# A graph layer on one core: the table of mean and rstd stored sooner, three gathers behind rstd, b_edge's products ahead of the attributes'

## What is computed

```python
h    = relu(layernorm(x))                         # mean and rstd of each row of x
edge_emb = edge_attr @ W_edge + b_edge
msg  = relu(h[src] + edge_emb)
aggr = segment_sum(msg, dst)
h1 = (1 + eps) * h + aggr
h1 = gelu(layer_norm(h1 @ W1 + b1)); h1 = gelu(layer_norm(h1 @ W2 + b2))
h1 = layer_norm(h + h1)
out = x + layer_norm(h1 + gelu(h1 @ M1) @ M2)
```

## Time and profile before

| | |
|---|---|
| median of three runs | 529.01 us |
| the profiled execution | 530.68 us |
| its span | 528.7 us |
| PE, DVE, ACT, POOL busy | 473.1, 392.8, 309.4, 282.0 us |
| head, up to the first z | 0 to 32.2 us |
| edge stage, first to last z | 32.2 to 276.5 us |
| node stages | some 280 to 528 us |

### The profile page before, as it was taken

The page is one execution under the profiler, slowest core; times in us unless marked ns, Lnnn a source line. Parts: engine busy times, 40 slices in busy tenths (PEclk is TensorE's granted clock), DMA queues, the critical chain, the costliest instruction groups (busy, mean ns, idle before and its releaser), DMA issues.

```text
span 528.7 us, 7255 instructions
## 1 busy us (share of the span) xinstructions
PE 473.1 (89%) x1930; PEld 345.0 (65%) x1930; DVE 392.8 (74%) x563; ACT 309.4 (59%) x584; POOL 282.0 (53%) x295
## 2 busy tenths in 40 slices
PE   1398998999689997799687999999999999999994
PEld 0034655666446664466455888888888889888884
DVE  7953969999478995768696577777999866672575
ACT  5643767998558986766893556555666656013000
POOL 5575776777758777667500344534554463330252
PEclk9999998999979999799999999999999999999999
DMA  8966877777767767667404733243551132130122
GB/s 272 332 181 190 304 265 246 232 244 221 210 213 217 226 213 239 187 195 242 133 9 137 264 91 116 92 160 99 159 160 40 61 86 73 40 116 4 40 80 80
DMA packets 31716, 85.52 MB, mean 162 GB/s; under 512 B 4880, under 2 KB 5216, under 8 KB 31648
## 3 DMA queue, kind: packets, MB, share of 16 engines
q0 software_dynamic: 12688, 41.17, 25.8%
q1 hardware_dynamic: 18960, 43.52, 25.2%
HBM read 72.08 MB, written 5.25 MB: 146 GB/s over the span
## 4 chain that ended last, share of the span: by engine, by line
PE 39%; DVE 28%; issue 9%; ACT 7%; another core or an unknown queue 5%; POOL 3%; DMA 3%; ACTq 3%; DVEq 2%; POOLq 0%; SPq 0%
DVE msg_lo L1084 12%; DVE z L1078 11%; PE ps_u L1282 8%; PE ps_u L1284 8%; PE ps_u L1283 8%; PE ps_t L1282 3%; PE ps_t L1284 3%; PE ps_t L1283 3%; PE ps_t L1455 2%; ACT msg_hi L769 2%; ACT apart L685 2%; DMA w_raw<-in_W 2%; PE ps_u L1295 2%; DVEq L1077 1%
## 5 line engine op out<-in xcount | busy, mean ns | idle before, releaser
L574 POOL DMA_INDIRECT rows<-gather_table,src_idx x153 | 169.9, 1110 | 63.6 <-issue 43.6
L769 ACT ACTIVATE msg_hi<-z 128x1024 fp32r<-128x1024 f32 (+1 forms) x79 | 82.6, 1046 | 39.2 <-DVE z L1078 24.1
L580 POOL TENSOR_TENSOR var_eps<-mv,eps_t 128x1 f32<-128x1 f32 x40 | 21.6, 539 | 144.4 <-ACT squares L827 86.0
L1078 DVE TENSOR_TENSOR z<-ps_u,rows 128x1024 f32<-128x1024 f32 (+1 forms) x53 | 64.3, 1213 | 43.3 <-remote 34.6
L1084 DVE SCALAR_TENSOR_TENSOR msg_lo<-z,msg_hi 128x1024 fp32r<-128x1024 f32 (+1 forms) x79 | 95.3, 1208 | 1.4 <-ACT msg_hi L769 0.8
L1299 PE MATMUL ps_u<-we_raw,attr_raw 128*128 128x512 f32 x130 | 69.7, 636 | 16.6 <-DVE z L1078 13.5
L1317 PE MATMUL ps_t<-msg_lo,onehot 128*128 128x512 f32 x149 | 65.6, 440 | 4.8 <-ACT ps_t L728 3.6
L1282 PE MATMUL ps_u<-w_hi,lhs_lo 128*128 128x512 f32 x160 | 64.5, 403 | 1.0 <-DVE lhs_lo L1126 1.0
L1284 PE MATMUL ps_u<-w_hi,lhs_hi 128*128 128x512 f32 x160 | 62.6, 392 | 0.0
L1283 PE MATMUL ps_u<-w_lo,lhs_hi 128*128 128x512 f32 x160 | 62.3, 390 | 0.0
L1317 PE MATMUL ps_t<-msg_hi,onehot 128*128 128x512 f32 x149 | 59.7, 401 | 0.0
(11 more groups left out here) (178 smaller groups left out, 1015.1 us busy)
## 6 DMA issues: line engine op xcount, KB each, us to landing
attr_raw<-in_attr_t SPq DMA_DIRECT2D x20, 512.0 KB
w_raw<-in_W SPq DMA_DIRECT2D x24, 256.0 KB, 3.0
tile_in<-mid SPq DMA_DIRECT2D x10, 512.0 KB, 3.6
res<-in_x SPq DMA_DIRECT2D x20, 256.0 KB, 2.7
xin<-in_x SPq DMA_DIRECT2D x5, 512.0 KB, 6.1
out<-work SPq DMA_DIRECT2D x10, 256.0 KB, 2.0
rows<-gather_table,src_idx POOLq DMA_INDIRECT x153
gather_table<-tab SPq DMA_DIRECT2D x4, 512.0 KB
```

The costliest lines, as they stand in the source:

```text
L574: g.indirect_dma_start(rows[:, group.r, e % TPG, :], None, gather_table[:, :], bass.IndirectOffsetOnAxis(src_idx[:, e:e + 1].bitcast(u32), ...
L769: a.activation(pair(msg_hi, g, p), summed(g, p), ACT.Relu).then_inc(msg_hi_done, 1)
L1078: v.tensor_tensor(summed(g, p), embedded(g, p), rows[:, g.r, 2 * p:2 * p + g.in_pair(p), :].rearrange("p a d -> p (a d)"), ALU.add).then_i ...
```

## The change

SP stores `node_stats` behind the second store of the table instead of the third. DVE makes `x_nbias` and `x_pair` behind tile 4 of the table instead of tile 6 (with their waits for all moments and all rstd). POOL gathers the first direct tile behind rstd of piece 1 as before, the other three behind the rstd of the last piece. ACT splits the first attributes ahead of the scale of `acc`, not behind it. PE makes the four products of `b_edge` in one go as soon as `b_edge` is there, ahead of its wait for `we_lo`, and the products of the attributes accumulate on them.

```diff
             for c in range(XC - 1):
                 save_tables(2 * c, 2)
-                if c == 2:
+                if c == 1:
                     sp.wait_ge(x_pair_ready, 1)
                     sp.dma_start(node_stats.rearrange("(p t) c -> p (t c)", p=P),
...
                 if c == 1:
                     pool.wait_ge(idx_in, 16)
-                if c >= 1:
-                    direct_rows(c - 1)
-
+                    direct_rows(0)
+
+            for e in range(1, DIRECT):
+                direct_rows(e)
             pool.wait_ge(stats_idx_ready, 1)
...
+            split_attr(fixed(0))
             act.wait_ge(eps1_ready, 1)
             act.wait_ge(x_rstd_done, XC)
             a.activation(acc_scale[:, :], x_rstd[:, :], ACT.Copy, scale=eps1[:, 0:1]).then_inc(acc_scale_ready, 1)
             act.wait_ge(acc_scale_ready, 1)
             act.wait_ge(nodes_ready, NT)
-            split_attr(fixed(0))
...
-                if i == 6:
+                if i == 4:
                     dve.wait_ge(x_moments, NT)
                     dve.wait_ge(x_rstd_done, XC)
...
                 o = embedded(g, p)
-                alone_in_bank = g.gr != 0 if isinstance(g.gr, int) else True
+                fresh = not (isinstance(g.gr, int) and g.gr == 0)
                 for e in range(g.in_pair(p) - 1, -1, -1):
-                    if not alone_in_bank:
-                        t.matmul(o[:, e * D:(e + 1) * D], ones[0:1, :], b_edge[0:1, :], start=True, stop=False)
...
             t.matmul(ps_t[0][:, 0:2 * ET], ones[:, :], span_diag[:, :], start=True, stop=True).then_inc(span_all_ready, 1)
+            pe.wait_ge(b_edge_in, 16)
+            for p in range(2):
+                for e in range(2):
+                    t.matmul(embedded(fixed(0), p)[:, e * D:(e + 1) * D], ones[0:1, :], b_edge[0:1, :], start=True, stop=True)
             pe.wait_ge(we_lo_ready, 1)
-            pe.wait_ge(b_edge_in, 16)
             embed(fixed(0), 0)
             embed(fixed(0), 1)
             embed(fixed(1), 0)
```

More of the change, by code:

```diff
@@ L1278, in _, with three @@
             t = nc.tensor
[L1280 to L1284, removed]
+            def three(o, lhs, cols, rhs, rcols, first, last, skip=False):
+                t.matmul(o, lhs[1][cols], rhs[0][rcols], start=first, stop=False, skip_group_check=skip)
+                t.matmul(o, lhs[0][cols], rhs[1][rcols], start=False, stop=False, skip_group_check=skip)
+                return t.matmul(o, lhs[0][cols], rhs[0][rcols], start=False, stop=last, skip_group_check=skip)
             def embed(g, p):
@@ L1299, in embed @@
                         last = t.matmul(o[:, e * D:(e + 1) * D], attr_raw[:, g.k, (2 * p + e) * P:(2 * p + e + 1) * P], we_raw[:, :],
-                                        start=alone_in_bank, stop=True)
+                                        start=fresh, stop=True, skip_group_check=not fresh)
                     else:
                         last = three(o[:, 0:D], (attr_hi[:, place, :], attr_lo[:, place, :]),
-                                     (slice(None), slice(part * P, (part + 1) * P)), (we_hi, we_lo), (slice(None), slice(0, D)), alone_in_bank, True)
+                                     (slice(None), slice(part * P, (part + 1) * P)), (we_hi, we_lo), (slice(None), slice(0, D)), fresh, True,
+                                     skip=not fresh)
                 last.then_inc(emb_done[p], 1)
```

## The result

The change made the kernel **slower**: 537.52 us (median of 4 runs, 532.06 to 538.61) against 529.17 us for the kernel before beside it (4 runs, 528.76 to 530.51), a ratio of 1.0116, 95% interval [1.0066, 1.0166]. The profiled execution took 538.05 us, its span 536.3 us against 528.7.

The account below looks back on a forecast made before the run. The prediction took the chain through PE's attribute products and a late PE signal at pair 3 to bound the head. Pair 3 starts 8.7 us sooner, within POOL's slack of 10.9: 529.01 - 8.7 = 520.3 us, range 515.3 to 524.8.

Parts of the forecast that it names:

- nothing behind pair 3 has a fixed time of its own: Edge stage: only POOL's gathers have a fixed time, so pair 3's gain of 8.7 us reaches the end.
- the price of POOL's three gathers is nothing: POOL's head: gathers run from 15 to 18.8 us, before the statistics arrive, covered even if each took 1 us more.
- PE's `b_edge` products: PE's head: four products of 2.0 us run from 13.0 to 21.0 us, and the attributes start at 21.4.
- 25.0, 28.4 and 31.4: PE's ends of pairs 0, 1 and 2 in us, instead of 29.8, 37.5 and 40.2.
- Row and rule: PE's clock: removing `b_edge` products from the run may bring 2.4 GHz sooner, pair 2 done 2 to 3 us earlier.
- Small table and store: Head: small store at 16.9 us, landed at 21.3; first statistics gather 22.0, first table gather 27.1, 2.4 us sooner.
- `begin` at 31.4: PE ahead of pair 3: `begin` starts when PE is free at 31.4 us; the plan's reading adds 0 to 2 us.
- If the late signal goes with PE's work: Pair 3: PE's late signal keeps its 7.05 us behind `begin`, so pair 3 starts at 41.1, 8.7 us sooner.
- rival A: Pair 3: late signal gone or harmless, start near 36 us, POOL caps the gain at 10.9: 518.1 us; chance 0.24.
- "no change" rival: Edge stage: a later release that goes by its own time swallows all the gain; chance 0.04.
- rival B: Late signals shift and take back part, or store and plan come late: 3 to 6 us gained, 523 to 526; chance 0.12.
- Rival C: Early edge stage: idle PE stays at the low clock, 2.6 us lost per pair, 533.3 us with five; chance 0.07.

Follow-up runs that it names:

- e10: The change without POOL's part (its three gathers stay between the rstd), against the kernel before: 527.65 us, ratio 0.9930.
- e6: The kernel before with POOL's part alone, three gathers behind the last rstd: 541.03 us, ratio 1.0189.
- e11: The changed kernel with every second table gather from pair 12 on replaced by a copy of one row: 494.74 us, one execution.
- e18: The kernel before with the odd tiles' table gathers from pair 12 on replaced by a copy of one row: 495.57 us, one execution.
- e1: The change without PE's part, against the kernel before at 498.49 us: 491.06 us, ratio 0.9848.
- e3: The changed kernel with POOL at most 4 pairs ahead of `z` instead of 6, against the kernel before at 498.49 us: 487.82 us, ratio 0.9780.
- e2: The kernel before with PE's part alone (`b_edge` products ahead), against the kernel before at 498.49 us: 499.30 us, ratio 0.9999.
- e17: The change itself measured again, against the kernel before at 530.32 us: 534.18 us, ratio 1.0100.
- e8: The changed kernel with POOL at most 4 pairs ahead of `z` instead of 6, against the kernel before at 530.88 us: 532.24 us, ratio 1.0001.
- e16: The changed kernel with all table gathers from pair 12 on cut to 512 of 2048 bytes a row, as many descriptors: 532.26 us.

## Why the prediction was wrong

I forecast 520.3 us (515.3 to 524.8) and gave slower 0.07; it was 537.52. Two steps failed: that nothing behind pair 3 has a fixed time of its own, and that the price of POOL's three gathers is nothing. By the ratios, the forecast gain of 8.7 us shrank to 3.7 in e10, where POOL's part is left out (0.9930), and to a loss of 6.1 with it (1.0116): about 5 us for the first step and 10 for the second. Step by step:

- **PE's `b_edge` products: right.** Done by 20.2 instead of 21.0, the attributes at 21.34 (forecast 21.4). They came out faster at the end than "25.0, 28.4 and 31.4", since PE's granted clock reached its 2.4 GHz level at 26 us (matmuls 0.23 us apart from 26.3 on): pair 2's record ended at 28.5. "Row and rule" had named that.
- **Small table and store: right.** Store at 16.63 (16.9), first statistics gather 22.82 (22.0, inside the bounds of 20.5 to 23.7), first table gather 27.84 (27.1), `z` of pairs 0 to 2 at 31.14, 33.39 and 34.52 (29.9, 31.9, 33.2). The small store took 5.5 us to land, where I had taken 4.4.
- **`begin` at 31.4: right by luck.** It came at 31.09, but not because PE was busy until then. PE was free at 28.5 and waited for the plan, made at 29.72, and for the reading of it (1.4 us), a term that I had left open as 0 to 2 us.
- **POOL's three gathers, "their price is nothing": wrong, and of the largest effect.** Hidden as time, they set the pattern of the 153 gathers behind them. Alone they cost 1.9% (e6), and all the rest gains 0.7% (e10): 1.0189 x 0.9930 = 1.0118, against 1.0116 for the whole change; that it agrees so closely is luck, as the intervals are 0.4 to 0.7% wide on each side. The prediction counted when instructions ran and not what state they left POOL in against DVE.
- **"If the late signal goes with PE's work" (41.1 us for pair 3): wrong.** Pair 3 had none and started at 37.00, rival A's figure of "near 36". The late signal came two pairs later. Its end goes with POOL's run: with pairs 3 and 4 done, POOL's limit moved out by two pairs. 18 gathers from 27.84, instead of 14 from 29.47, end at 50.73 instead of 47.48. Pair 5 started about 3 us after that, at 53.89. The 7.05 us were no length of PE's own; that three runs agreed fits a stop of POOL that recurs just as well.
- **"Nothing after pair 3 has a fixed time of its own except POOL's gathers": wrong; here the head's gain was lost.** Where a late signal ends with POOL's stop, it does have a time of its own, set by POOL's start and buffers. It swallowed the gain at pair 5: 1.2 us were left in the changed kernel, 1.0 in e11 against e18. The "no change" rival had the shape ("a release later in the edge stage that goes by its own time swallows all") and I wrote "I see none", with 0.04.
- **The loss itself** (from 1.2 us ahead at pair 5 to 7.8 behind at the end) is rival B's mechanism, releases grown by several us, at a size I had not allowed: waits of about 4 us, most of them 6 to 8 pairs apart, from pair 11 on. Rows 7 had shown 11 waits and 34.6 us of the unseen sort. By the count above they grew by a third (32.7 to 44.4 us behind pair 5), which is already more than the 8.7 us offered; I let B only take back part.
- **Rival C was not it**, though its sign is there. From 57.5 us on matmul records stand 0.42 us apart, behind the wait of 9.8 us, and from 30 to 60 us the granted clock was 0.83 against 0.94. But `z` of pairs 5 and 6 are 2.49 us apart there, so DVE still set the pace. Between 60 and 240 us PE was at its full level as much as before, 0.96 against 0.95, and the gap ahead of `begin` (28.5 to 31.1 us) did not end the high level that had begun at 26 us.

In condition 499 the forecast's direction holds: e1 gains 1.5% and e3 2.2%, but not by its mechanism. There POOL, slowed by meeting DVE, bounds the kernel before, and e1, with the new order, is free of that; pair 3 alone gains nothing (e2). The change itself was not run in that condition.

**What stays open.** Why the issue of indirect gathers delays PE's signals, why that differs between two occasions on one chip, and what starts a late signal after 15 to 21 us of POOL's run in the new pattern, while in the old one POOL goes up to 65 us. Nor is POOL's pause the whole rule for their end: in e17 the `z` of 46.33 us, after 6.6 us of waiting, went before any pause of POOL, and so did those of 142.02 and 209.34 us in the kernel before. Why POOL's order makes the late signals more numerous, a wider pitch of the gathers, and a kernel that gathers without POOL were not tried or are not known.

**A better version.** In condition 530 e10, the change without POOL's part, beats both kernels: by 0.7% the one before and by 1.7 to 1.9% the change (0.9930 against 1.0096 to 1.0116, measured at different times). In condition 499 the change with a lead of 4 (e3) gains 2.2%, and the same kernel is level in condition 530 (e8, 1.0001). No version was found best in both (e10 itself was not run in condition 499); of those run in both, e3's loses in neither.

## What to carry to other kernels

A wait whose releaser isn't in the trace is not to be moved along with the engine it is put down to: look what the other engines do when it ends, at all its places, and work the new time out from that. Where one recurs, ask of an engine sped up whether these waits get more numerous, and let the range hold a growth of their sum; here it was a third. An instruction hidden in time isn't free if a long periodic run of its engine begins behind it; time it alone, and time the kernel before again beside every measurement, for one kernel here (e3, e8) was worth 2.2% in one condition of the machine and nothing in the other.

## What the runs showed of the hardware

- While POOL issued indirect gathers 1.25 us apart, without a pause, PE's signals came late, on DVE and on SP alike: in the changed kernel a product whose records end at 44.55 us let SP go at 54.06, and in e16 PE's last record ended at 96.85 and `z` went at 99.67. With half of the gathers left out from pair 12 on, the later waits are gone (494.74 and 495.57 us against 530 to 537); with a quarter of the bytes they are not (532.26).
- The same kernel before takes 530 or 499 us, 6%, and the late signals are in every profile of the one condition and in none of the other. The chip numbered 0 had both.
- An indirect gather of 128 rows took POOL 0.95 us. If it started while DVE was in `msg_lo` or `attr_lo`, it took longer by the time for which that instruction still ran, less 0.13 us (up to 1.96 us). Which pattern of meetings sets in was decided by three gathers 10 us before, and made 12.9 us of difference in POOL's gathers (169.9 us in the kernel before, 157.0 in e6).
